# A decoder layer's hand-written order of work: projections of a batch spread to 9 to 11 places, router rows away from a group's output, the second batch's rows behind the first maximum tiles

## What is computed

```python
x = x + attn(layernorm(x), ...)              # 16 heads of 16; causal; rotary turn on half of each head
x = x + xattn(layernorm(x), ctx, ctx, mask)  # 16 heads of 16; keys and values from ctx (8, 512, 256)
x = x + ffn(layernorm(x), router, w1, b1, w2, b2)  # 8 experts of width 1024; each takes its 512 best rows
return x
```

## Time and profile before

| | us |
|---|---|
| median of 3 runs | 1296.25 |
| lowest and highest | 1288.26 and 1298.76 |
| profiled execution, its own time | 1295.45 |
| its span in the trace | 1293.7 |
| first "st" of group 0 | 75.3 after the span's start |
| attention ends, mixture begins | about 1010 |

### The profile page before, as it was taken

The page is one execution under the profiler, slowest core; times in us unless marked ns, Lnnn a source line. Parts: engine busy times, 40 slices in busy tenths (PEclk is TensorE's granted clock), DMA queues, the critical chain, the costliest instruction groups (busy, mean ns, idle before and its releaser), DMA issues. The chain is left out here.

```text
span 1293.7 us, 21922 instructions
## 1 busy us (share of the span) xinstructions
PE 1144.6 (88%) x7616; PEld 683.2 (53%) x7616; DVE 969.7 (75%) x2633; ACT 713.2 (55%) x1429; POOL 530.1 (41%) x728
## 2 busy tenths in 40 slices
PE   5699999999999999999999999999996218999994
PEld 2454545555455554544445454545333217888984
DVE  6678788788888778888888887878861577666551
ACT  6035555545555556676767676666773104565561
POOL 4656375654758443434242424240212003454332
PEclk9669899899999999999999999999999558999997
DMA  5551533515335243342525252415110504454322
GB/s 169 114 116 33 117 85 80 115 35 131 84 99 126 91 115 98 102 100 81 116 66 116 66 115 67 99 54 112 34 42 25 185 4 164 111 112 119 98 26 25
DMA packets 89330, 117.94 MB, mean 91 GB/s; under 512 B 12065, under 2 KB 59105, under 8 KB 89090
## 3 DMA queue, kind: packets, MB, share of 16 engines
q1 hardware_dynamic: 83074, 107.97, 32.5%
q0 software_dynamic: 6144, 8.52, 4.0%
HBM read 48.63 MB, written 16.91 MB: 51 GB/s over the span
## 5 line engine op out<-in xcount | busy, mean ns | idle before, releaser
L785 ACT ACTIVATE probs<-ps_st 128x512 f32<-128x512 f32 (+3 forms) x1024 | 476.5, 518 | 269.6 <-PE ps_st L618 265.6
L638 PE MATMUL ps_p<-kst,qst 63*128 63x512 f32 (+3 forms) x1024 | 383.5, 436 | 9.7 <-DVE mx L895 8.0
L618 PE MATMUL ps_st<-qst,kst 64*128 64x512 f32 (+3 forms) x1024 | 360.1, 419 | 9.2 <-ACT probs L785 8.4
L893 DVE TENSOR_REDUCE mx<-ps_p 128x1 f32<-128x512 f32 x512 | 322.3, 681 | 43.0 <-PE ps_p L638 42.2
L618 PEld LDWEIGHTS ps_st<-qst,kst 64*128 64x128 f32 x1024 | 165.9, 187 | 261.7 <-ACT probs L785 199.9
L895 DVE CUSTOM_DVE_ANT_0 ps_p<-ps_p,tri 128x128 f32<-128x128 f32 (+3 forms) x512 | 238.1, 515 | 13.7 <-PE ps_p L638 12.6
L599 PE MATMUL ps_o<-probs,vals 128*32 128x512 f32 (+3 forms) x2048 | 234.4, 530 | 14.6 <-POOL probs L508 14.6
L638 PEld LDWEIGHTS ps_p<-kst,qst 63*128 63x128 f32 x1024 | 172.5, 189 | 35.3 <-DVE mx L895 15.8
L450 POOL TENSOR_SCALAR lnw<-mv 128x4 f32<-128x4 f32 x24 | 5.1, 211 | 337.1 <-DVE mv L879 337.0
L508 POOL TENSOR_SCALAR_AFFINE_SELECT probs<-probs 128x512 f32<-128x512 f32 x128 | 79.2, 635 | 85.9 <-ACT probs L785 85.5
L1278 PE MATMUL moe_ps_y<-moe_w,moe_hid_h 128*128 128x256 f32 x512 | 94.6, 283 | 0.0
(11 more groups left out here) (224 smaller groups left out, 1893.5 us busy)
## 6 DMA issues: line engine op xcount, KB each, us to landing
qst<-qk_h SPq DMA_DIRECT2D x64, 256.0 KB, 4.7
kst<-qk_h SPq DMA_DIRECT2D x64, 256.0 KB, 4.9
qst<-qk_l SPq DMA_DIRECT2D x32, 256.0 KB, 5.4
kst<-qk_l SPq DMA_DIRECT2D x32, 256.0 KB, 4.9
moe_w1r<-in_w_dram SPq DMA_DIRECT2D x8, 1024.0 KB, 5.0
moe_w2r<-in_w_dram SPq DMA_DIRECT2D x8, 1024.0 KB, 9.9
xin<-in_x_dram SPq DMA_DIRECT2D x8, 512.0 KB, 4.1
xres<-in_x_dram SPq DMA_DIRECT2D x8, 512.0 KB, 3.9
```

What stands on the lines that cost most here:

```text
L618: last = nc.tensor.matmul(out, kst[rows, t % 2, pair, kt * P:(kt + 1) * P], qst[rows, t % 2, pair, lo:S], start=True, stop=not masked)
L638: last = nc.tensor.matmul(ps_p1[:, i % 3, 0:keys], qst[rows, t % 2, pair, qt * P:(qt + 1) * P], kst[rows, t % 2, pair, 0:keys], start=True ...
L785: nc.scalar.activation(probs[:, kt, j, 0:n], ps_st[:, i % 2, 0:n], ACT.Exp, scale=float(DH) ** -0.5).then_inc(exp_done, 1)
L893: nc.vector.tensor_reduce(mx[:, g % 2, at:at + 1], bank, AX.X, ALU.max).then_inc(max_done, 1)
```

## The change

The steps keep what they compute; they change places. In a batch's projections the places 35, 43, 51, 59 become 35, 44, 55, 64, so the last falls into the next turn, behind its first "st" and "p1". "v" 1 moves from 15 to 16; "y" from 27 and 31 to 28 and 32. The router rows "xt3" move from 47 and 47 to 51 and 52, "lg" from 55 and 67 to 59 and 68. For batch 1 "ln" moves from -68 to -63, "xt" from -47 and -46 to -26 and -25, "qk" from -45, -28, -21, -14 to -22, -17, -13, -8. `fourth` moves from behind "xt" of batch 1 to behind "v" of batch 0.

```diff
@@ program()
-        put(far - 4 if t == 1 else far + 10, "ln", t)
-        put(far + (17 if t == 1 else 23), "xt", t, 0)
-        put(far + (18 if t == 1 else 27), "xt", t, 1)
+        put(far + 1 if t == 1 else far + 10, "ln", t)
+        put(far + (38 if t == 1 else 23), "xt", t, 0)
+        put(far + (39 if t == 1 else 27), "xt", t, 1)
         for i in range(4):
-            put(far + ((19, 36, 43, 50) if t == 1 else (35, 43, 51, 59))[i], "qk", t, i // 2, i % 2)
+            put(far + ((42, 47, 51, 56) if t == 1 else (35, 44, 55, 64))[i], "qk", t, i // 2, i % 2)
             put(far + (65, 66, 75, 76)[i], "stack", t, i // 2, i % 2)
         put(near + 11, "v", t, 0)
-        put(near + 15, "v", t, 1)
+        put(near + 16, "v", t, 1)
...
-        put(after + 27, "y", t, 0)
-        put(after + 31, "y", t, 1)
+        put(after + 28, "y", t, 0)
+        put(after + 32, "y", t, 1)
...
-            put(after + 47, "xt3", t, 0)
-            put(after + 47, "xt3", t, 1)
-            put(after + 55, "lg", t, 0)
-            put(after + 67, "lg", t, 1)
+            put(after + 51, "xt3", t, 0)
+            put(after + 52, "xt3", t, 1)
+            put(after + 59, "lg", t, 0)
+            put(after + 68, "lg", t, 1)
@@ VectorE's start
-            fourth = STEPS.index(("xt", 1, 1)) + 1
+            fourth = STEPS.index(("v", 0, 1)) + 1
...
-            run(STEPS[fourth:])
+            run([s for s in STEPS[fourth:] if s not in statistics])
```

## The result

| | before | after |
|---|---|---|
| median (4 runs each), us | 1293.88 | 1355.21 |
| lowest and highest | 1288.26 and 1298.76 | 1353.57 and 1361.22 |
| ratio, 95% interval | | 1.048 (1.043 to 1.054) |
| profiled execution, own time | 1295.45 | 1353.57 |
| its span | 1293.7 | 1351.8 |

The forecast was 1300.7, within 1% of no change, with a range of 1286 to 1310; the change is 45 us slower than the range allows. Of the 58.1 us between the two spans, 57.2 lie ahead of the last maximum tile. I measured each turn from the start of the first tile of its place 0 to that of the next turn. Turns 0 to 7 took 43.6 us more in all, turns 8 to 15 took 13.4 more, and the start 0.2.

The account below looks back on a forecast made before the run. TensorE was taken to set the pace, so reordering could win only its idle time. Start +1.5, projections +8.1, start of turn 6 +0.8, router rows -5.1 gave +5.3 on 1295.45: 1300.7 us, range 1286 to 1310.

Parts of the forecast that it names:

- The three projections that move within a turn: Turns 0 to 5: stalls at 62 and 70 go, new ones at 54 and 74; +1.35 us a turn, +8.1 in all.
- Maximum tiles that queue behind the eviction: Self-attention turns, before "pv" at 62: tiles wait behind VectorE's eviction of a projection, taking back 0.1 to 0.4 us.
- Rival 2: Clock falls more often in self-attention stretches without a projection: three or more extra dips, 3.4 us each, 1311 us; 15%.
- v, y, store: Moves one place later: no bank nearer than 4 places, "store" still finds "y" done; cost nothing.
- In cross-attention the projections' own moves cost nothing: Cross-attention turns: no "pv" waits for a triangle there, so moving the projections costs nothing.
- Router rows: Cross-attention and turn 15: transposes no longer wait for VectorE's scaled output; -5.1 us (-6 to 0).
- The start: Before the first "st": batch 1's rows and projections placed among the first maximum tiles; +1.5 us (-2.7 to +2.7).

Follow-up runs that it names:

- e5: Kernel before with only the projections of batches 2 to 15 moved, to places 35, 44, 55, 64: 1340.43 us, ratio 1.040.
- e10: Kernel before with only the fourth projection moved, from place 59 to 64: 1333.23 us, ratio 1.031.
- e4: Kernel before with only "v" 1 moved from 15 to 16 and "y" from 27 and 31 to 28 and 32: 1302.04 us, ratio 1.009.
- e3: Kernel after with each step it puts at an even place moved one place later, to an odd one: 1325.45 us, ratio 1.025.
- e9: Kernel before with only the third projection of batches 2 to 15 moved, from place 51 to 55: 1326.06 us, ratio 1.028.
- e6: Kernel before with only the router rows moved, "xt3" to 49 and 53, "lg" to 57 and 67: 1295.53 us, ratio 1.002.
- e7: Kernel before with only the start changed (batch 1's places and VectorE's `fourth`): 1295.65 us, ratio 1.002.
- e12: Kernel before with projections of batches 2 to 7 at 37, 45, 53, 61, each directly behind a triangle instruction: 1310.47 us, ratio 1.014.

## Why the prediction was wrong, step by step

- **"The three projections that move within a turn", +8.1 us.** The step that failed: e5 gives +48. Its stalls were right in place. "pv" at 54 came 6.26 us behind that at 46, as before (6.27), so it was pinned as forecast, but idled 0.64 us where 1.5 were forecast, because TensorE had already waited 0.45 us for ScalarE at place 52; the two make 1.09. At 46 a wait of 0.34 us for ScalarE came ahead, and the stall for the triangle was 0.35 in place of 0.86. Those at 62 and 70 went; that at 74 was 1.18 against 1.1. Wrong was the belief that a turn's length follows from its stalls: idle time per turn rose by about 1.1 us, as forecast, and the turn by 8, since TensorE's busy time rose by 6.9. The term had the clock's falls and the places' own cost at nothing.
- **"Maximum tiles that queue behind the eviction", 0.1 to 0.4 us.** They were 0.50 + 0.21 + 0.21 us at places 59 to 61, just where the fourth projection had stood. e10 shows that opening that stretch is enough for the clock to fall.
- **Rival 2, the clock, 15% and 3 x 3.4 us.** This was the largest part, and its count was far too low: three falls of 6.8 us beyond the present ones were priced, and 68 us more at low clock came, ten such falls, two in most turns. Its price for one fall was too high (3.4 us for 6.8; measured 2.0 to 2.9). The rows had the warning: the two dips of the earlier trace rows stood behind a stall in a stretch with no projection, and the change makes two such stretches in every turn. A third dip, at 481, was overlooked; it too stands behind a wait of TensorE (1.22 us for VectorE, at 479.8). I counted turns 1, 3, 4 and 5, that had the same stall and no dip, as evidence against; seen from the result they were near to one. The Trainium skill's section "A second HAM failure mode: psum-queue depth-cycling" of "TensorE: Matmul & The Clock Gate" describes TensorE idling for moments between groups of matmuls until the clock swings between its two levels; the trace agrees, with waits of 0.2 to 1.2 us and a low clock behind them.
- **"v, y, store: nothing".** Wrong by 11 us (e4). I looked for banks and found none near. The cost has no wait: for the smaller part it is the overlap of two score tiles, lost at the even places 16, 28 and 32; the larger part stays at odd places (e3) and is, as far as is known, the overlap with the small product that stood at the same place.
- **"In cross-attention the projections' own moves cost nothing".** Wrong: e5's cross-attention turns are 2.2 us longer. The third projection alone costs 1.2 of these (e9) and the fourth 0.6 (e10), with waits for ScalarE where a projection has left.
- **Router rows, -5.1 us.** The wait went as forecast, the time did not (e6: +0.2%). Behind it ScalarE was late next, for a third of it.
- **The start, +1.5 us.** Too small by half: it is some 3 us (e7, and the first "st" over all traces), just over the upper bound of 2.7. The times themselves came as forecast, first tile 48.77 against 49.2, first "st" at 75.5 against 77, as these rows of TensorE show. The key mask and the early load of batch 2 cost nothing that can be seen. The low clock of the start is not one piece: before, it was at full speed from 54.4 to 57.8.

```profile
48.77 1.47 PE L638 MATMUL ps_p<-kst,qst 63*128 63x128 f32 x4 [9.63 <-DMA kst<-qk_h]
...
75.51 0.40 PE L618 MATMUL ps_st<-qst,kst 64*128 64x512 f32 x1
```

What remains of the 61 us beside the clock's 20 to 29 and about 11 for "v" and "y" is some 21 to 30 us: some 3 us of the start, the parted tiles and lost neighbours of the moved projections and router rows, the stall at 74, and waits for VectorE and ScalarE in the stretches that lost a projection. These were not separated further. Open too is why e9 and e12 have their falls only in every second turn. The runs show only that added matmuls keep the falls off and that a stretch that lost its product can bring them; e12 leaves the projections 8 places apart and has falls too, so it isn't the only way to them.

## What to carry to other kernels

Where an engine is busy nine tenths of its time, the waits listed for it are not a sum to be collected: ask what each small product hides at the place where it stands, and what is late next once the wait is gone (e6, e12). Before spreading work out, find the stretches that it leaves thin: if the clock has dipped there even twice in sixteen turns, price the change with a dip in every turn as one of its cases. A single execution can mislead by its clock: the four of e5 lie 17.6 us apart. And where products overlap with their neighbours, a move of one place is not free (e4): leave small products side by side, and put them between pairs of tiles and not within one.

## What the runs showed of the hardware

- A small product over all 128 rows that moved by one place, from beside another small product to between two score tiles of different row halves, cost 0.15 to 0.40 us with no wait in the trace (turn 10 of e4). At the odd place next to it the three together still cost 0.60 of 0.88 us (e3 against the change).
- The granted clock fell to 1.2 GHz in stretches in which TensorE idled only in pieces of 0.2 to 1.2 us, such as the places ahead of 366 in turn 4 of the kernel after. 6.8 us at low clock cost 2.4 to 2.5 us and not 3.4. In the kernel before, turn 3 has such a fall and turn 4 has none: TensorE was busy 52.6 and 50.0 us and idle 3.0 and 3.1, so the waits stayed and the work grew by less than half of the fall. The work does not all take twice as long: eight "pv" of 512 columns took 1.93 us for 1.06, a score tile of 512 columns 0.79 for 0.50 (kernel after, 366.98 and 370.72).
- Executions of one kernel differ by their falls: 0.29 to 0.37 us for each us more at low clock (19 of the kernel before, four of e5).
- Forty-two matmuls that compute nothing, put into the thin places, made the changed kernel 17 us faster, and the kernel before 12 us slower.
